# Turning the context rows by DMA instead of TensorE in a gated cross-attention decoder

## The reference, cut to what matters

```python
x = x + tanh(g_xattn[0]) * L0_xattn(ctx, ctx, layernorm(x), ...)     # long convolution
x = x + tanh(g_ffn[0])   * L0_ffn(layernorm(x), ...)                 # shared + 8 routed experts, top 2
x = x + tanh(g_xattn[1]) * L1_xattn(layernorm(x), ctx, Wq, Wg, bg, Wkv, Wo)
x = x + tanh(g_ffn[1])   * L1_ffn(layernorm(x), ...)                 # soft mixture of 16 experts

def L1_xattn(query, kv, Wq, Wg, bg, Wkv, Wo):       # 16 heads of 32
    q    = feature(query @ Wq.T);  gate = sigmoid(query @ Wg.T + bg)
    k, v = split(kv @ Wkv.T);      k = feature(k)   # feature(t) = t + 1 if t > 0 else exp(t)
    summary, k_sum = sum_s k v^T,  sum_s k          # per head, over the 256 tokens of a sequence
    return (q @ summary / (q @ k_sum + eps)) * gate @ Wo.T
```

## Time and profile before

| what | value |
|---|---|
| time, median of 3 runs | 1770.28 us (1766.94 to 1773.11) |
| time of the profiled execution | 1764.81 us |
| its span | 1762.9 us |
| PE busy, share of the span | 1565.1 us, 89% |
| DVE busy | 1092.9 us, 62% |
| ACT busy | 757.6 us, 43% |
| POOL busy | 513.8 us, 29% |
| mean granted clock of TensorE | 0.957 of full speed |

### The profile page before, as it was taken

One profiled execution on the slowest core, in us unless ns is written; L12 is line 12 of the kernel. 1 busy time (PEld: TensorE's weight loads), 2 busy tenths in 40 slices (PEclk: granted clock), 3 DMA queues, 4 the chain that ended last, 5 costly groups with the idle time before them and its releaser, 6 DMA issues. The chain is left out here.

```text
span 1762.9 us, 27544 instructions
## 1 busy us (share of the span) xinstructions
PE 1565.1 (89%) x9484; PEld 908.1 (52%) x9484; DVE 1092.9 (62%) x2221; ACT 757.6 (43%) x1393; POOL 513.8 (29%) x428
## 2 busy tenths in 40 slices
PE   4989948999799999679898876889999999999997
PEld 3778833444356566435454442545555555555554
DVE  7998845335623333268685864766676767575663
ACT  5443214333123333134343451656564656566462
POOL 0657824333324444234342331120202010101101
PEclk7999969999999999889999997989999999999999
DMA  9545544645596887552434215624250505142241
GB/s 206 145 118 151 160 149 134 199 146 153 172 222 168 242 210 193 196 197 77 151 90 163 70 64 217 220 68 84 49 118 20 125 18 113 38 93 57 63 89 44
DMA packets 293579, 228.83 MB, mean 130 GB/s; under 512 B 197778, under 2 KB 241298, under 8 KB 291170
## 3 DMA queue, kind: packets, MB, share of 16 engines
q1 hardware_dynamic: 244912, 156.73, 34.7%
q10 hardware_dynamic: 39298, 40.54, 8.0%
q0 software_dynamic: 9264, 30.15, 5.6%
HBM read 125.58 MB, written 54.87 MB: 102 GB/s over the span
## 5 line engine op out<-in xcount | busy, mean ns | idle before, releaser
L2127 POOL TENSOR_TENSOR s_h_lo<-s_h,s_h_hi 128x512 f16<-128x512 f32 x32 | 37.0, 1155 | 550.9 <-DVE s_h_hi L2329 550.9
L2347 PE MATMUL s_ring<-w_mu,s_xt_hi 128*128 128x512 f16 x256 | 99.5, 389 | 7.0 <-DVE s_xt_lo L2250 3.8
L1275 DVE TENSOR_TENSOR e_h<-e_up,e_silu 128x352 f32<-128x352 f32 x39 | 20.4, 524 | 137.0 <-ACT e_silu L1220 137.0
L2255 DVE TENSOR_REDUCE s_top<-s_lg 128x1 f32<-128x512 f32 x64 | 43.9, 686 | 92.7 <-ACT s_lg L2169 92.5
L2348 PE MATMUL s_ring<-w_mu,s_xt_hi 128*128 128x512 f16 x256 | 99.3, 388 | 0.0
L2349 PE MATMUL s_ring<-w_mu,s_xt_lo 128*128 128x512 f16 x256 | 99.1, 387 | 0.0
L2347 PE MATMUL s_acc<-w_w,s_g_hi 128*128 128x512 f16 x256 | 97.1, 379 | 0.2
L2347 PE MATMUL s_ring<-w_w,s_xt_hi 128*128 128x512 f16 x256 | 97.0, 379 | 0.0
L2348 PE MATMUL s_ring<-w_w,s_xt_hi 128*128 128x512 f16 x256 | 97.0, 379 | 0.0
L2349 PE MATMUL s_ring<-w_w,s_xt_lo 128*128 128x512 f16 x256 | 97.0, 379 | 0.0
L2349 PE MATMUL s_acc<-w_w,s_g_lo 128*128 128x512 f16 x256 | 97.0, 379 | 0.0
(11 more groups left out here) (387 smaller groups left out, 4780.8 us busy)
## 6 DMA issues: line engine op xcount, KB each, us to landing
expert_rows<-e_y SPq DMA_DIRECT2D x39, 256.0 KB, 2.8
a_part_in<-in_L_ffn_W ACTq DMA_DIRECT2D x32, 256.0 KB, 3.2
w_split<-a_part_q ACTq DMA_DIRECT2D x32, 256.0 KB, 2.5
w_w<-w_split SPq DMA_DIRECT2D x8, 1024.0 KB, 21.9
toep<-ssm_split ACTq DMA_DIRECT2D x14, 512.0 KB, 5.2
stage<-in_L_ffn_gate_w SPq DMA_DIRECT2D x8, 704.0 KB, 4.4
stage<-in_L_ffn_up_w SPq DMA_DIRECT2D x8, 704.0 KB
xattn_w_split<-e_part_q ACTq DMA_DIRECT2D x20, 256.0 KB
```

The source lines that it names most:

```text
L2255: V.tensor_reduce(top[:, t, j:j + 1], lg[:, t, j * D:(j + 1) * D], AX.X, ALU.max).then_inc(S["top_done"], 1)
L2347: mm(out_, a[0], b_[0], start=first, stop=False)
```

## The change

The context tile is split into halves as it lies, with tokens on the partitions. ACT writes the hi half into a new buffer `cq` straight from `ctx_in`, DVE subtracts it from `ctx_in` and writes the lo half beside it. Then SP issues one transposing DMA per tile, 128 x 1024 fp16 elements (256 KB), from `cq` into `ct_all`, which holds both turned halves. TensorE's TC transposes go, and TC leaves the ring of banks; K and V wait on the DMA's semaphore.

```diff
-        ct = tuple(sb(f"a_ct_{q}", [P, KD, CH], F16) for q in ("hi", "lo"))
+        ct_all, cq = sb("a_ct", [P, 2 * KD, CH], F16), sb("a_cq", [P, 4, 2, D], F16)
+        ct = (ct_all[:, 0:KD, :], ct_all[:, KD:2 * KD, :])
...
-        READ = {"TC": (c_lo, 4), "TX": (x_lo, 4), "K": (feat_done, 8), ...
+        READ = {"TX": (x_lo, 4), "K": (feat_done, 8), ...
...
+            def turn_context(c):
+
+                if c:
+                    sp.wait_ge(v_done, c * 4)
+                for t in range(4):
+                    sp.wait_ge(c_lo, c * 4 + t + 1)
+                    sp.dma_start_transpose(ct_all[:, :, t * P:(t + 1) * P], cq[:, t].rearrange("p q d -> p (q d)")).then_inc(c_turned[t], 16)
+
             def load_next(c):
 
-                sp.wait_ge(c_turned, 4 * c + 4)
+                sp.wait_ge(c_lo, 4 * c + 4)
                 sp.dma_start(ctx_in[:, :, :], ctx_d[:, c * 4 + 4:c * 4 + 8, :]).then_inc(ctx_loaded, 16)
                 load_rows(c + 1)
...
             for n in range(5):
                 if n == 1:
+                    turn_context(0)
                     load_rows(0)
                 if n == 3:
                     load_next(0)
...
             for c in range(NCH):
                 if 0 < c < NCH - 1:
                     load_next(c)
+                if c < NCH - 1:
+                    turn_context(c + 1)
                 if c == NCH - 2:
 
-                    sp.wait_ge(c_turned, NCH * 4)
                     sp.wait_ge(stored, c * 4 * 16)
...
                 if op == "TC":
-                    act.wait_ge(c_turned, c * 4 + n + 1)
+                    act.wait_ge(ctx_loaded, (c + 1) * 16)
                     if c:
 
-                        act.wait_ge(v_done, c * 4)
-                    A(ct[0][:, :, n * P:(n + 1) * P], ring[:, bank, :].rearrange("p (k i) -> p k i", i=P), ACT.Copy).then_inc(c_hi, 1)
+                        act.wait_ge(c_turned[n], c * 16)
+                    A(cq[:, n, 0, :], ctx_in[:, n, :], ACT.Copy).then_inc(c_hi, 1)
...
+                if op == "TC":
+                    dve.wait_ge(c_hi, c * 4 + n + 1)
+                    V.tensor_tensor(cq[:, n, 1, :], ctx_in[:, n, :], cq[:, n, 0, :], ALU.subtract).then_inc(c_lo, 1)
...
-                if op == "TC":
-                    pe.wait_ge(ctx_loaded, (c + 1) * 16)
-                    turn(bank, ctx_in, n).then_inc(c_turned, 1)
...
                 if op in ("K", "V"):
                     o = op == "V"
-                    pe.wait_ge(c_lo, c * 4 + n + 1)
+                    pe.wait_ge(c_turned[n], (c + 1) * 16)
                     pe.wait_ge(w_loaded[o], 16)
```

More of the change, by code:

```diff
@@ L1401, in xattn_phase @@
         first_added, combined, normed = sem("a_first_added"), sem("a_combined"), sem("a_normed")
-        c_turned, c_hi, c_lo = sem("a_c_turned"), sem("a_c_hi"), sem("a_c_lo")
+        c_turned, c_hi, c_lo = [sem(f"a_c_turned{t}") for t in range(4)], sem("a_c_hi"), sem("a_c_lo")
         x_turned, x_hi, x_lo = sem("a_x_turned"), sem("a_x_hi"), sem("a_x_lo")
@@ L1444, in xattn_phase @@
         w2_out = w2_split.rearrange("j p (q e d) -> j e p q d", q=2, e=JE)
-        READ = {"TC": (c_lo, 4), "TX": (x_lo, 4), "K": (feat_done, 8), "Q": (feat_done, 8), "V": (v_lo_done, 4), "G": (gate_exp, 4),
+        READ = {"TX": (x_lo, 4), "K": (feat_done, 8), "Q": (feat_done, 8), "V": (v_lo_done, 4), "G": (gate_exp, 4),
                 "SM": (kv_done, 4), "AT": (weighted_done, 8), "OUT": (out_read, 4)}
@@ L1730, in step @@
                     V.tensor_scalar(ah.rs[:, :], ah.rs[:, :], ah.scl[:, 0:1], None, ALU.mult).then_inc(AS["rs_done"], 1)
-                if op in ("TC", "TX"):
-                    hi_done, lo_done, dst = (c_hi, c_lo, ct) if op == "TC" else (x_hi, x_lo, xt)
+                if op == "TC":
+                    dve.wait_ge(c_hi, c * 4 + n + 1)
+                    V.tensor_tensor(cq[:, n, 1, :], ctx_in[:, n, :], cq[:, n, 0, :], ALU.subtract).then_inc(c_lo, 1)
+                if op == "TX":
                     tok = slice(n * P, (n + 1) * P)
-                    dve.wait_ge(hi_done, c * 4 + n + 1)
-                    V.tensor_tensor(dst[1][:, :, tok], ring[:, bank, :].rearrange("p (k i) -> p k i", i=P), dst[0][:, :, tok],
-                                    ALU.subtract).then_inc(lo_done, 1)
+                    dve.wait_ge(x_hi, c * 4 + n + 1)
+                    V.tensor_tensor(xt[1][:, :, tok], ring[:, bank, :].rearrange("p (k i) -> p k i", i=P), xt[0][:, :, tok],
+                                    ALU.subtract).then_inc(x_lo, 1)
                 if op == "K":
```

## The result

| | before | after |
|---|---|---|
| time, median | 1768.61 us (4 runs) | 1782.91 us (4 runs, 1780.85 to 1787.86) |
| ratio to before, 95% interval | | 1.0078 [1.0052, 1.0103] |
| profiled execution, its span | 1764.81, 1762.9 us | 1781.48, 1779.7 us |
| mean granted clock of TensorE | 0.957 | 0.946 |

A forecast was written before the change was run, and what follows sets the result against it. The prediction took a DVE-ACT circle, not TensorE, to bound stage 1. It summed +5.5 (opening) + 4.7 (DVE held by POOL) - 2.2 (turn 2's stall) = +8.0 us on 1770.3, giving 1778.3 us, range 1774 to 1784 (wider: 1767 to 1788).

The forecast's parts named there:

- the three terms: Whole kernel: +5.5 us for the opening's transposes, +4.7 for DVE waiting on POOL, -2.2 for turn 2's load wait.
- What bounds the kernel: Stage 1: a circle of DVE and ACT sets the pace, 5.93 us a round, against TensorE's 5.6.
- The opening: Phase start: four transposes ahead of `wv`, 1.38 us each, delay it by 5.5 us; bounds 2.7 and 9.
- DVE held by POOL: Stage 1, turns 0 to 2: context's lo half waits for POOL's subtraction, nine rounds of 0.52 us, +4.7 us.
- Turn 2's stall: Turn 2, stage 1: TensorE no longer waits for the context load, so the late gate goes, -2.2 us.
- SP in steady state: Turns 0 to 2: SP's waits for the halves and its transposing DMAs delay nothing needed soon, price 0.
- The clock's rival: Turns 0 to 2: TensorE idles before AT, its clock drops, V reaches DVE late; +6 us, 1784, chance 0.1.

The follow-up runs named there:

- the last version: Changed kernel, all turns by DMA, with POOL's first gathers waiting for the transposes and turns 1 and 2's loads ahead of the stores; 1764.66 us, 0.9956.

## Why the prediction came out as it did

The forecast was 1778.3 us, its own range 1774 to 1784; measured were 1782.9. The sign and the signs of the three terms held; the largest term was half of what it should be. That the time still lies inside the range owes something to luck. As differences the range is +3.7 to +13.7 us, and the measured one is +13.8 (+14.3 by the medians), at or past its edge; the kernel before came out at 1768.6 in place of 1770.3. Two further terms were off the other way or missing, and nearly cancelled.

**What bounds the kernel: right.** DVE with ACT sets stage 1. The run that keeps the turns on TensorE shows it: from the first CB to the norm of the next chunk turns 0 and 1 take 22.8 us each with four turns in them and 22.8 without. TensorE's wait ahead of the first AT of turn 1 grew from 2.04 to 8.60 us instead. The Trainium skill (VectorE: DVE Perf Modes, Rules for kernel authors) prefers TensorE for a 128x128 block where PSUM can take it. With chunk 0 on TensorE and on the DMA engines the times were 1.000 and 1.0078, which agrees, but with the gathers held back the DMA way measured 1.0012, so most of that difference is not the DMA way's own.

**The opening, +5.5: the path right, the term mis-sized; it measured +11.3,** outside its own bound of 9. The step that failed reads "All that was moved before `wv` must still be moved, and the transposes go in between", priced by four transposes "in a stretch with nothing else moved". It took the engines' time as a sum of shares, each at its price alone. That doesn't hold here, since x and `wv` stand behind the transposes, and what runs beside them is the gathers: then a gather's packet takes 0.54 us instead of 0.14 and the four transposes 18.9 instead of 7.7. With the transposes moved behind `wv`, where nothing is slowed, V came 5.2 later and Q 3.7. The excess of this term, 5.8 us, is as large as the gap between 8.0 predicted and 13.8 timed, but it isn't the whole story of it: the hold was 1.4 too large, the clock brought 1.8 that the sum lacks, and the start of CB moved by another 0.5. No row of the kernel before showed transposes and gathers together, so the bound from above was not one.

The Trainium skill (Advanced Engine Details and Errata, X-Bar Transpose) gives 350 to 400 GB/s. The traces do not agree: 190 GB/s alone, 233 GB/s in the 3 us shown of the run with the transposes behind `wv`, and beside gathers 0.10 MB in 3 us for the transposes.

**DVE held by POOL, +4.7: right in mechanism, too large.** From the first CB to the norm, stage 1 grew by 1.5 us in turn 0 (1.6 expected) and by 0.9 in turn 1; turn 2 takes after the change what turn 1 takes, so 0.9 there too, 3.3 in all. The prediction took turn 0's pace for all turns, but in turns 1 and 2 a round was 6.02 us before, and only 0.31 is added to it. Alone in the kernel before the hold gives +1.4 and +0.9 in turns 0 and 1. The Trainium skill (SBUF — State Buffer, section SBUF: two separate sides) states such a rule: of a DVE instruction with two SBUF inputs and a GpSimd one that reads SBUF, the first to start has the ports they share until its end, and the other is blocked. The trace agrees: DVE's lo half starts inside POOL's part and ends 0.55 us behind it.

**Turn 2's stall, -2.2: right.** Turn 2 lost 2.1 us with the hold inside it: -2.2 for the stall, +0.9 for the hold, and -0.7 because its first CB came earlier after Q, where the prediction had it no earlier. Turn 1 had a cost that the prediction lacks: DVE waits for x of the next chunk at 880.52:

```profile
880.52 0.75 DVE L1695 SCALAR_TENSOR_TENSOR a_x<-a_y,mix,a_x 128x512 f32<-128x512 f32 x1 [2.69 <-DMA a_x<-after_shared]
```

Before, this wait was 0.53 us, on top of TensorE's stall. CB starts 1.2 us later after Q than it did. SP issued the turn's first transpose at 877.91 (1.25 us) while x, asked for at 871.30, was still landing. In this profile that may have slowed it: x landed 4.1 us behind the context, where it was 2.6 before. It can't be the whole cause. In the second profile of after x landed 9.7 us after it was asked for (9.2 in the first, 8.0 before), but the context ahead of it had already landed late, 7.7 us after its issue against 5.9, before the first transpose was issued. With chunk 0 on TensorE it was 10.1 and 8.0 in the same way. Why the context lands late there is open.

**SP in steady state, 0:** stage 3 of no turn waits for a turned tile. Right, apart from what the transpose may do to x in turn 1.

**The clock's rival was half there.** V didn't come late for DVE, as it had it. The clock moved in stage 4 instead, -1.6 in turn 0 and +1.7 in turns 1 and 2, +1.8 in all.

**What stays open.** The ledger closes for the profiled pair: 11.3 + 1.5 + 2.1 - 2.1 - 1.6 + 3.4 = 14.6 of 14.7 us. For the kernel with chunk 0 on TensorE it doesn't: its phase is 5.4 and 3.7 us longer than before in two profiles, its time the same in two timings (0.9998, 1.0001). What lies outside the phase varies between profiles from 1413.4 to 1418.9 us with the same code, before itself at both ends of that, so one profile can't settle 3 us. It is the same with others: with the gathers late the phase is 5.2 us longer and the time 2.1, with the transposes behind `wv` 8.9 and 4.4, and of the 7.8 us of the last version the phase shows 2.4. So the size of a single term is known to within some us only. And whether the timed runs have the long stage 4 as often as the profiled ones wasn't seen. What decides stage 4's clock is open too.

## What to carry to other kernels

Before a transfer is put ahead of others in a queue, list what will run beside it once the others are held back: a price taken from a stretch where it ran alone is no upper bound. Moving work off a busy engine pays only where that engine ends the wait; here its neighbour's queue order, edited alone, gave 0.3% that the change itself could not. When an operand moves from PSUM to SBUF on DVE, look at what POOL is doing at that moment.

## What the hardware showed that was not expected

- Four transposing DMAs of 256 KB hold SP for 7.7 and 7.1 us without POOL's gathers, 18.9 and 18.6 beside them; 212 GB/s over that stretch with the engines' shares adding to over 1. Both sides get through less, and the gather's packets take 3.8 times as long.
- SP's time on an issue does not tell by itself that a transfer is slow: 18.03 us for the four when queued behind plain loads, while those ran at 388 GB/s. The count of packets under 512 B by window tells when the transposes move.
- Stage 4's clock, 1.00 or 0.82 of full speed with the same matmuls, mostly repeats from execution to execution of a kernel and moves to other turns with small changes elsewhere. It fell behind a wait of 2.43 us in one kernel and stayed at 1.00 behind the same wait in another.
